# Two attention phases on one core: value products in groups of four tiles behind every second step, in place of two behind each

## The chip, the cores and the metric

One Trainium2 chip, one of its cores. The engines of the core run their own instruction lists and meet through semaphores: TensorE (PE in the profile, its weight loads apart as PEld), VectorE (DVE), ScalarE (ACT), GpSimd (POOL) and SyncE (SP), which issues the transfers. The metric is the time of one launch on the device in microseconds; lower is better.

## The reference, cut to what matters

Four layers run one after the other over x (16 batches of 256 tokens, width 128). Layers 0, 2 and 3 are attention layers with 16 heads of 8 channels; layer 1 is a mixture of three experts and is not touched here.

```python
# layers 0 and 3: self attention (256 keys), then cross attention (1601 keys) and an MLP
# layer 2: cross attention (1601 keys) with adaptive layer norms
attn_w = softmax(einsum('bhqd,bhkd->bhqk', q, k) * hd ** -0.5)
attn_out = einsum('bhqk,bhkd->bhqd', attn_w, v)
x = x + gate * (attn_out @ W_proj + b_proj)
```

All is computed in float32 and softmax runs over all keys.

## The kernel before, in words

`layers` calls five programs in a row: a small modulation stage, the attention phase `pa` (layer 0), the expert layer, and the attention phase `pb` (layers 2 and 3). This case is about `attention_phase`.

A phase carries two **streams**: "c", cross attention with 1601 keys (13 key tiles of 128, the last of 65), and "z", self attention with 256 keys (2 tiles). Each item of a stream is one batch of one layer. The phase is a list of **bodies**; each body does the scores and value products of one item of c and, where the streams overlap, one item of z, beside the preparation of later items and the finish of earlier ones. `pa` has 16 items each of c and z, z four bodies ahead: 12 bodies with both, 4 with c alone, 4 with z alone. `pb` has 32 items of c and 16 of z, z four bodies behind: 16 bodies with both, 16 with c alone.

The heads are taken in four **quads** of four. A quad is a row of **macro steps**: six of c with two key tiles each (tokens `("S", q, j, pp)`, two units per step), one of c for the last tile (`("T", q)`), and one of z (two tiles), eight steps in all or seven without z. The work around a step:

- *Scores* (S, T; L890, L898): four bf16 matmuls of 64 rows, two at a time on the two halves of the array, into one of two `aunit` buffers (`RING_A = 2`). ACT takes the exponential of the whole 128x1024 buffer into one of six `probs` buffers (L668) and so frees the `aunit`.
- *Value products* (V; L914): per key tile four products, one per head, each with 9 columns of weights (8 channels and a column of ones for the denominator) in its own strip of 32 columns of the array, against a 256 column float32 `probs`. Every product appears as two matmuls in the trace, so a tile is 8 of them. They add up in the bank `obank`, c in the left half and z in the right. The first tile of a quad waits until the quad before has been moved out: `wait(pe, o_ev, out_before[...])`, L905 of the kernel.
- *Moving out* (`oev`; L676): after the last tile of a quad ACT copies each stream's half of `obank` to `osb`.
- *Maxima* (M; L927 and L599): for the next item, PE computes the scores once more the other way round into one of three `dbank` buffers (`RING_D = 3`) and DVE reduces each to row maxima. 56 units of c and 8 of z per body, each of two buffers.
- *Helpers*: transposes of the context (`ctx`), key, query and value projections (`k`, `q`, `v`), output transposes (`o`), projections and the MLP, each once per item, in places given by hand.

The order is the same on every engine: `body_plan` gives each token a position between 0 and 1 in the body and sorts; `stage_list` repeats the plan for all bodies; every engine walks that list and does its share. In `body_plan` the list `main` holds score units (cost 1) and groups of values (cost: their number of tiles), spread evenly; the maxima units are spread evenly by their width on their own, and the helpers have fixed positions.

## Time and profile before

| | us |
|---|---|
| median of 3 runs | 5992.55 |
| lowest, highest | 5966.28, 6003.84 |
| the profiled execution | 5973.85 |
| its span | 5972.1 |

PE is busy 84% of the span, DVE 68%, ACT 62%. PE's busy time counts a matmul from its start to its end, while the next one is already streaming, so it is not a measure of how full the array is. In pb a body with both streams takes 99.3 us and one with c alone 88.6 us, from the first exponential of one to that of the next; the quads inside are unequal, since most helpers sit in the first two. In the rows below, windows show the busy time of each engine in a stretch, the timeline shows merged instructions in order of time with the idle time before them and what ended it, and the waits show who waited for whom.

### The profile page before, as it was taken

How to read it: one execution, taken by the hardware profiler on the slowest of the kernel's cores; microseconds unless marked ns; L12 is line 12 of the kernel's file. 1: busy time of each engine (PE TensorE's matmuls, PEld its weight loads, DVE VectorE, ACT ScalarE, POOL GpSimd, SP SyncE). 2: the span in 40 equal slices, each digit the busy share in tenths (PEclk: the TensorE clock that was granted, in tenths of full speed). 3: DMA queues.
4: the chain of work that ended last, by engine and by line, in shares of the span. 5: the costliest groups of instructions: out<-in, count | busy, mean ns of one | idle time of the engine just before them, and what ended most of it. 6: DMA issues, size and time to landing. Idle time of an engine off the chain costs nothing.

```text
span 5972.1 us, 124563 instructions
## 1 busy us (share of the span) xinstructions
PE 5013.7 (84%) x48593; PEld 2443.0 (41%) x48593; DVE 4034.0 (68%) x8799; ACT 3691.2 (62%) x5043; POOL 1624.9 (27%) x2594
## 2 busy tenths in 40 slices
PE   3688888888888688888598888888888898888887
PEld 1233333333433466666233333333334343333333
DVE  3487877777776233332588878787877777777774
ACT  1376767667767233332277777777777777777775
POOL 2434343343321000000423232323222322322321
PEclk8699999999999788888699999999999999999998
DMA  1221111211110100000211212121212111111110
GB/s 42 60 61 46 51 53 50 59 43 47 51 34 24 34 16 22 23 23 17 68 43 58 60 50 61 50 61 50 61 50 62 48 51 44 52 49 42 53 42 7
DMA packets 362968, 271.18 MB, mean 45 GB/s; under 512 B 47905, under 2 KB 324990, under 8 KB 362384
## 3 DMA queue, kind: packets, MB, share of 16 engines
q1 hardware_dynamic: 362384, 263.23, 15.5%
q8 instruction: 387, 6.34, 0.4%
q14 instruction: 197, 1.61, 0.1%
HBM read 86.96 MB, written 12.78 MB: 17 GB/s over the span
## 4 chain that ended last, share of the span: by engine, by line
PE 31%; DVE 8%; ACT 6%; POOL 4%; issue 4%; SPq 0%; DMA 0%; ACTq 0%; POOLq 0%
PE pb_obank L914 11%; PE pb_dbank L927 7%; DVE pb_c_maxs L599 6%; ACT pb_probs L668 4%; PE pb_aunit L890 4%; PE pb_aunit L961 2%; PE pb_aunit L968 2%; POOL pb_c_cin L789 1%; PE pb_aunit L1001 1%; PE pb_dbank L975 1%; DVE pb_z_maxs L599 1%; POOL pb_c_hg L852 1%; PE pb_aunit L995 1%; POOL pb_c_cs_y L785 0%; ACT pb_c_ksp L712 0%
## 5 line engine op out<-in xcount | busy, mean ns | idle before, releaser
L599 DVE TENSOR_REDUCE pb_c_maxs<-pb_dbank 128x1 f32<-128x512 f32 (+1 forms) x3584 | 2050.6, 627 | 633.3 <-PE pb_dbank L927 621.2
L668 ACT ACTIVATE pb_probs<-pb_aunit 128x1024 f32<-128x1024 f32 (+1 forms) x1792 | 1756.0, 1025 | 460.7 <-PE pb_aunit L890 364.6
L599 DVE TENSOR_REDUCE pa_c_maxs<-pa_dbank 128x1 f32<-128x512 f32 (+1 forms) x1792 | 1028.6, 627 | 395.6 <-PE pa_dbank L927 390.4
L668 ACT ACTIVATE pa_probs<-pa_aunit 128x1024 f32<-128x1024 f32 (+1 forms) x960 | 943.0, 1025 | 263.6 <-PE pa_aunit L890 190.8
L927 PE MATMUL pb_dbank<-pb_c_kst,pb_c_qst 62*128 62x512 bf16 (+1 forms) x4096 | 880.1, 343 | 141.5 <-DVE pb_c_maxs L599 77.0
L914 PE MATMUL pb_obank<-pb_probs,pb_c_vaug 128*9 128x256 f32 x13312 | 890.2, 382 | 6.6 <-ACT pb_probs L668 6.5
L890 PE MATMUL pb_aunit<-pb_c_qst,pb_c_kst 64*128 64x256 bf16 x6144 | 595.8, 273 | 53.3 <-ACT pb_probs L668 21.9
L927 PEld LDWEIGHTS pb_dbank<-pb_c_kst,pb_c_qst 62*128 62x128 bf16 x4096 | 248.6, 93 | 778.4 <-DVE pb_c_maxs L599 563.7
L927 PE MATMUL pa_dbank<-pa_c_kst,pa_c_qst 62*128 62x512 bf16 (+1 forms) x2048 | 449.0, 354 | 61.5 <-DVE pa_c_maxs L599 24.2
L914 PE MATMUL pa_obank<-pa_probs,pa_c_vaug 128*9 128x256 f32 x6656 | 461.2, 393 | 0.8 <-ACT pa_probs L668 0.7
L914 PEld LDWEIGHTS pb_obank<-pb_probs,pb_c_vaug 128*9 128x9 f32 x13312 | 276.1, 90 | 371.9 <-issue 177.3
L890 PEld LDWEIGHTS pb_aunit<-pb_c_qst,pb_c_kst 64*128 64x128 bf16 x6144 | 258.6, 95 | 242.0 <-ACT pb_probs L668 84.4
L890 PE MATMUL pa_aunit<-pa_c_qst,pa_c_kst 64*128 64x256 bf16 x3072 | 300.9, 278 | 25.7 <-ACT pa_probs L668 16.7
L927 PEld LDWEIGHTS pa_dbank<-pa_c_kst,pa_c_qst 62*128 62x128 bf16 x2048 | 123.3, 95 | 390.0 <-DVE pa_c_maxs L599 257.1
L599 DVE TENSOR_REDUCE pa_z_maxs<-pa_dbank 128x2 f32<-128x512 f32 x256 | 164.1, 686 | 115.3 <-PE pa_dbank L927 113.9
L1506 POOL TENSOR_TENSOR moe_xo<-moe_y,moe_xin 128x256 f32<-128x256 f32 x16 | 11.6, 723 | 844.2 <-DVE moe_y L1412 844.2
L914 PEld LDWEIGHTS pa_obank<-pa_probs,pa_c_vaug 128*9 128x9 f32 x6656 | 140.2, 91 | 195.7 <-issue 101.7
L803 POOL TENSOR_TENSOR pb_c_kf<-pb_c_kf,pb_c_ksp 128x1024 f32<-128x1024 f32 x64 | 114.3, 1787 | 311.1 <-ACT pb_c_ksp L712 311.1
L890 PEld LDWEIGHTS pa_aunit<-pa_c_qst,pa_c_kst 64*128 64x128 bf16 x3072 | 129.1, 96 | 117.3 <-ACT pa_probs L668 44.2
L599 DVE TENSOR_REDUCE pb_z_maxs<-pb_dbank 128x2 f32<-128x512 f32 x256 | 164.6, 685 | 10.5 <-PE pb_dbank L927 8.7
L1564 PE MATMUL moe_bank_f<-moe_diag,moe_pr 128*128 128x128 f32 (+1 forms) x832 | 136.9, 320 | 35.5 <-DVE moe_pt L1255 28.5
L1456 ACT ACTIVATE moe_pr<-moe_bank_s,moe_nm 128x400 f32<-128x400 f32 (+1 forms) x128 | 74.3, 594 | 132.5 <-DVE moe_nm L1337 132.5
(460 smaller groups left out, 6864.7 us busy)
## 6 DMA issues: line engine op xcount, KB each, us to landing
pb_c_kst<-pb_c_ksp SPq DMA_DIRECT2D x384, 200.1 KB
pa_c_kst<-pa_c_ksp SPq DMA_DIRECT2D x192, 200.1 KB
pb_c_cin<-in_ctx SPq DMA_DIRECT2D x32, 768.0 KB
pa_c_cin<-in_ctx SPq DMA_DIRECT2D x16, 768.0 KB
moe_cin<-in_ctx SPq DMA_DIRECT2D x16, 768.0 KB
pb_c_qst<-pb_c_qsp SPq DMA_DIRECT2D x384, 32.0 KB
pa_z_qst<-pa_z_qsp SPq DMA_DIRECT2D x192, 32.0 KB
pa_z_kst<-pa_z_ksp SPq DMA_DIRECT2D x192, 32.0 KB
```

The source lines that it names most:

```text
L599: dve.tensor_reduce(dst, dbank[N % RING_D][:, 0:cnt * width].rearrange("p (s c) -> p s c", s=cnt), AX.X, ALU.max).then_inc(d_free, 1)
L668: act.activation(probs[u % RING_P][0:rows].rearrange("p a i q -> p (a i q)"), src[0:rows, :], ACT.Exp, scale=HD ** -0.5).then_inc(a_free, 1)
L789: pool.tensor_scalar(s.cin[0:rows, t, :], s.cin[0:rows, t, :], s.cs_m[0:rows, t:t + 1], s.cs_y[0:rows, t:t + 1], ALU.add, ALU.mult).then_i ...
L803: pool.tensor_tensor(s.kf[:, part], s.kf[:, part], s.ksp[:, 0, part], ALU.subtract).then_inc(s.k_r, 1)
L852: pool.tensor_tensor(s.hg[:], s.hg[:], s.z[:], ALU.mult).then_inc(s.g_p, 1)
L890: ins = pe.matmul(dst[:, par * 512 + h * NQ:par * 512 + (h + 1) * NQ], s.kst[b2][lo:lo + ROWS, pair, t * P:(t + 1) * P], s.qst[b2][lo:lo + ...
L914: ins = pe.matmul(obank[32 * h4:32 * h4 + HD + 1, half * NQ:(half + 1) * NQ], s.vaug[i % 2][:, t, 4 * q + h4, :], src, start=(t == 0), sto ...
L927: ins = pe.matmul(dbank[nd[tok, s.key, i, par] % RING_D][:, col:col + width], s.qst[b2][lo:lo + MAX_ROW, p, qt * P:(qt + 1) * P], s.kst[b2 ...
L961: ins = pe.matmul(dst[:, at - t0 * P:at - t0 * P + width], w.wkp[:], src[:, at:at + width], start=True, stop=True)
L968: ins = pe.matmul(dst[0:rows, (t - t0) * P:(t - t0 + 1) * P], (s.srct if s.has_ctx else s.xmt)[:, t * P:t * P + rows], w.wv[:], start=True ...
L1456: act.activation(pr[qt][:, at:at + width], sbank[c][:, 0:width], ACT.Exp, bias=nm[:, qt:qt + 1], scale=D ** -0.5, accum_out=sums[:, qt, c: ...
L1564: ins = pe.matmul(dst[0:rows, (t - t0) * P:(t - t0 + 1) * P], pr[qt][:, t * P:t * P + rows], diag[qt][:], start=True, stop=True)
```

## The change

The group of values that stood behind the scores of each macro step (those of the step before) now stands behind the scores of every second step only and holds the values of the two steps before it. At even steps there is none. With eight steps a quad, the four groups of a quad hold: the two z tiles of the quad before and c's tiles 0 and 1; tiles 2 to 5; tiles 6 to 9; tiles 10 to 12. The tokens that move `obank` out (`oev`) stay right behind the last values of their quad, and so come to stand between the z tiles and tile 0 of the next quad. Nothing else is edited; the number of instructions is the same (17525 rows on PE in both).

```diff
--- before.py
+++ after.py
@@ -235,13 +235,16 @@
     for m, (s, units, _, _) in enumerate(macros):
         main += [[(s, 0, t)] for t in units]
         costs += [1.0] * len(units)
-        prev, _, vals, ends = macros[m - 1]
-        off = 0 if m else -1
-        group = [(prev, off, t) for t in vals]
-        if ends is not None:
-            group += [(o, off, ("oev", ends)) for o in streams]
-        main.append(group)
-        costs.append(len(vals))
+        group = []
+        for back in ((2, 1) if m % 2 else ()):
+            prev, _, vals, ends = macros[m - back]
+            off = 0 if m >= back else -1
+            group += [(prev, off, t) for t in vals]
+            if ends is not None:
+                group += [(o, off, ("oev", ends)) for o in streams]
+        if group:
+            main.append(group)
+            costs.append(sum(1 for g in group if g[2][0] == "V"))
     for pos, group in spread(main, 0.0, 1.0, costs):
         marks += [(pos, item) for item in group]
 
```

Place 1, PE, at the border of two quads in a body of pb with both streams. `pb_obank` is the bank of the values, `pb_aunit` takes scores, `pb_dbank` maxima. Before:

```order
L914 MATMUL pb_obank<-pb_probs2,pb_z_vaug1 9x256 x2
L914 MATMUL pb_obank<-pb_probs3,pb_z_vaug1 9x256 x2
L914 MATMUL pb_obank<-pb_probs2,pb_z_vaug1 9x256 x2
L914 MATMUL pb_obank<-pb_probs3,pb_z_vaug1 9x256 x2
L927 MATMUL pb_dbank0<-pb_c_kst0,pb_c_qst0 128x512
L927 MATMUL pb_dbank1<-pb_c_kst0,pb_c_qst0 128x512
L890 MATMUL pb_aunit1<-pb_c_qst0,pb_c_kst0 128x256 x4
L890 MATMUL pb_aunit0<-pb_c_qst0,pb_c_kst0 128x256 x4
L975 MATMUL pb_dbank2<-pb_ident,pb_c_osb 128x128 x4
L927 MATMUL pb_dbank0<-pb_c_kst0,pb_c_qst0 128x512
L927 MATMUL pb_dbank1<-pb_c_kst0,pb_c_qst0 128x512
L914 MATMUL pb_obank<-pb_probs4,pb_c_vaug0 9x256 x2
```

Now (the lines of the kernel have moved down by three, so L914 is L917 and so on):

```order
L893 MATMUL pb_aunit1<-pb_c_qst0,pb_c_kst0 128x256 x4
L893 MATMUL pb_aunit0<-pb_c_qst0,pb_c_kst0 128x256 x4
L930 MATMUL pb_dbank0<-pb_c_kst0,pb_c_qst0 128x512
L930 MATMUL pb_dbank1<-pb_c_kst0,pb_c_qst0 128x512
L917 MATMUL pb_obank<-pb_probs2,pb_z_vaug1 9x256 x2
L917 MATMUL pb_obank<-pb_probs3,pb_z_vaug1 9x256 x2
L917 MATMUL pb_obank<-pb_probs2,pb_z_vaug1 9x256 x2
L917 MATMUL pb_obank<-pb_probs3,pb_z_vaug1 9x256 x2
L917 MATMUL pb_obank<-pb_probs4,pb_c_vaug0 9x256 x2
L917 MATMUL pb_obank<-pb_probs5,pb_c_vaug0 9x256 x2
L917 MATMUL pb_obank<-pb_probs4,pb_c_vaug0 9x256 x2
L917 MATMUL pb_obank<-pb_probs5,pb_c_vaug0 9x256 x2
```

The z tiles and the next quad's tiles 0 and 1, which had two maxima units and two score units between them, are now neighbours, and the score units have gone ahead of both.

Place 2, ACT, at the same border; `osb` is what `obank` is moved to. Before:

```order
L668 ACTIVATE pb_probs4<-pb_aunit1 128x1024
L668 ACTIVATE pb_probs5<-pb_aunit0 128x1024
L676 ACTIVATE pb_c_osb<-pb_obank 128x256
L676 ACTIVATE pb_z_osb<-pb_obank 128x256
L668 ACTIVATE pb_probs0<-pb_aunit1 128x1024
L668 ACTIVATE pb_probs1<-pb_aunit0 128x1024
```

Now:

```order
L671 ACTIVATE pb_probs4<-pb_aunit1 128x1024
L671 ACTIVATE pb_probs5<-pb_aunit0 128x1024
L671 ACTIVATE pb_probs0<-pb_aunit1 128x1024
L671 ACTIVATE pb_probs1<-pb_aunit0 128x1024
L679 ACTIVATE pb_c_osb<-pb_obank 128x256
L679 ACTIVATE pb_z_osb<-pb_obank 128x256
L671 ACTIVATE pb_probs2<-pb_aunit1 128x1024
```

The two moves out stood behind the two exponentials of the quad's first step; they now stand behind all four of its first two steps.

Place 3, PE, in the middle of a quad of the same phase. Before:

```order
L890 MATMUL pb_aunit1<-pb_c_qst0,pb_c_kst0 128x256 x4
L914 MATMUL pb_obank<-pb_probs3,pb_c_vaug0 9x256 x2
L914 MATMUL pb_obank<-pb_probs4,pb_c_vaug0 9x256 x2
L914 MATMUL pb_obank<-pb_probs3,pb_c_vaug0 9x256 x2
L914 MATMUL pb_obank<-pb_probs4,pb_c_vaug0 9x256 x2
L927 MATMUL pb_dbank0<-pb_c_kst1,pb_c_qst1 128x512
L927 MATMUL pb_dbank1<-pb_c_kst1,pb_c_qst1 128x512
L890 MATMUL pb_aunit0<-pb_c_qst0,pb_c_kst0 128x256 x4
L890 MATMUL pb_aunit1<-pb_c_qst0,pb_c_kst0 128x256 x4
L927 MATMUL pb_dbank2<-pb_c_kst1,pb_c_qst1 128x512
L927 MATMUL pb_dbank0<-pb_c_kst1,pb_c_qst1 128x512
L914 MATMUL pb_obank<-pb_probs5,pb_c_vaug0 9x256 x2
```

Now:

```order
L893 MATMUL pb_aunit1<-pb_c_qst0,pb_c_kst0 128x256 x4
L930 MATMUL pb_dbank2<-pb_c_kst1,pb_c_qst1 128x512
L930 MATMUL pb_dbank0<-pb_c_kst1,pb_c_qst1 128x512
L917 MATMUL pb_obank<-pb_probs3,pb_c_vaug0 9x256 x2
L917 MATMUL pb_obank<-pb_probs4,pb_c_vaug0 9x256 x2
L917 MATMUL pb_obank<-pb_probs3,pb_c_vaug0 9x256 x2
L917 MATMUL pb_obank<-pb_probs4,pb_c_vaug0 9x256 x2
L917 MATMUL pb_obank<-pb_probs5,pb_c_vaug0 9x256 x2
L917 MATMUL pb_obank<-pb_probs0,pb_c_vaug0 9x256 x2
L917 MATMUL pb_obank<-pb_probs5,pb_c_vaug0 9x256 x2
L917 MATMUL pb_obank<-pb_probs0,pb_c_vaug0 9x256 x2
L930 MATMUL pb_dbank1<-pb_c_kst1,pb_c_qst1 128x65
```

Two groups of four rows with scores and maxima between them have become one of eight; the maxima that stood between now stand all on the other side.

## Rows read from the trace of the kernel before

**Rows 1.** windows, four quads of one body with both streams; columns in the first line.

```profile
core 0: us, PE busy (x) PEld busy (x) DVE busy (x) ACT busy (x) POOL busy (x), PEclk, DMA share, GB/s
3999.80:4029.90 30.10, 26.82 (x285) 13.61 (x281) 24.14 (x63) 20.13 (x29) 7.37 (x15) 1.00 0.37 111
4029.90:4057.90 28.00, 23.11 (x249) 9.76 (x244) 19.60 (x48) 21.37 (x29) 17.34 (x33) 1.00 0.05 15
4057.90:4079.10 21.20, 19.34 (x228) 7.61 (x228) 18.14 (x33) 16.51 (x21) 6.16 (x5) 1.00 0.28 75
4079.10:4099.10 20.00, 18.23 (x228) 7.16 (x224) 18.68 (x36) 15.78 (x19) 1.14 (x6) 1.00 0.04 9
```

**Rows 2.** windows, four quads of one body with the long stream alone.

```profile
5248.20:5272.50 24.30, 22.05 (x237) 10.91 (x232) 18.00 (x41) 16.33 (x22) 6.67 (x14) 1.00 0.36 114
5272.50:5298.80 26.30, 21.51 (x222) 9.40 (x217) 17.49 (x32) 19.69 (x25) 8.25 (x9) 1.00 0.00 1
5298.80:5319.50 20.70, 18.44 (x212) 8.33 (x208) 16.00 (x30) 14.67 (x18) 9.10 (x9) 1.00 0.24 64
5319.50:5336.80 17.30, 15.90 (x193) 5.93 (x190) 16.03 (x31) 13.11 (x16) 0.57 (x3) 1.00 0.04 9
```

**Rows 3.** timeline, last quad of rows 1; columns: start, length, engine, work, idle before.

```profile
4079.10 1.94 ACT L668 ACTIVATE pb_probs<-pb_aunit 128x1024 f32<-128x1024 f32 x2 [0.27 <-PE pb_aunit L890]
...
4079.73 0.55 PEld L914 LDWEIGHTS pb_obank<-pb_probs,pb_z_vaug 128*9 128x9 f32 x16 [0.23 <-issue]
...
4080.71 0.10 PEld L927 LDWEIGHTS pb_dbank<-pb_c_kst,pb_c_qst 62*128 62x128 bf16 x2 [0.43 <-DVE pb_c_maxs L599]
...
4080.92 0.39 ACT L676 ACTIVATE pb_c_osb<-pb_obank 128x256 f32<-128x256 f32 x1
...
4081.14 2.48 DVE L599 TENSOR_REDUCE pb_c_maxs<-pb_dbank 128x1 f32<-128x512 f32 x4 [0.22 <-PE pb_dbank L927]
4081.18 0.41 ACT L676 ACTIVATE pb_z_osb<-pb_obank 128x256 f32<-128x256 f32 x1
...
4081.88 0.09 PEld L927 LDWEIGHTS pb_dbank<-pb_c_kst,pb_c_qst 62*128 62x128 bf16 x1 [0.52 <-DVE pb_c_maxs L599]
...
4082.20 1.05 PE L914 MATMUL pb_obank<-pb_probs,pb_c_vaug 128*9 128x256 f32 x16
4083.18 0.12 PEld L927 LDWEIGHTS pb_dbank<-pb_z_kst,pb_z_qst 62*128 62x128 bf16 x4 [0.43 <-DVE pb_c_maxs L599]
...
4083.61 1.29 DVE L599 TENSOR_REDUCE pb_z_maxs<-pb_dbank 128x2 f32<-128x512 f32 x2
```

**Rows 4.** waits, the last two quads of rows 1: waiter, awaited, us, times, longest.

```profile
PEld pb_dbank L927 <- DVE pb_c_maxs L599: 12.3, 29, 1.0
...
DVE pb_c_maxs L599 <- PE pb_dbank L927: 4.1, 9, 1.6
```

**Rows 5.** waits, the first two quads of rows 1.

```profile
DVE pb_c_maxs L599 <- PE pb_dbank L927: 13.3, 12, 2.1
```

**Rows 6.** timeline of weight loads, a visit of one tile and the load after it.

```profile
4097.71 0.12 PEld L914 LDWEIGHTS pb_obank<-pb_probs,pb_c_vaug 128*9 128x9 f32 x8 [0.23 <-issue]
4098.26 0.09 PEld L927 LDWEIGHTS pb_dbank<-pb_c_kst,pb_c_qst 62*128 62x128 bf16 x1 [0.43 <-DVE pb_c_maxs L599]
```

**Rows 7.** instructions of tile pb_obank: count, ns min/median/max, first and last start.

```profile
L914 PE MATMUL pb_obank<-pb_probs,pb_z_vaug x1024: 379/379/385, 3332.7 to 4887.3; 128*9 128x256 f32 x171
```

**Rows 8.** the page, part 5: the exponentials of pb.

```profile
L668 ACT ACTIVATE pb_probs<-pb_aunit 128x1024 f32<-128x1024 f32 (+1 forms) x1792 | 1756.0, 1025 | 460.7 <-PE pb_aunit L890 364.6
```

**Rows 9.** waits, the last two quads of rows 2.

```profile
DVE pb_c_maxs L599 <- PE pb_dbank L927: 5.6, 10, 2.5
```

**Rows 10.** windows, nine bodies of pa with both streams.

```profile
306.00:1301.00 995.00, 865.18 (x9187) 385.41 (x9183) 757.60 (x1646) 700.88 (x920) 370.69 (x620) 0.96 0.19 53
```

**Rows 11.** timeline of the second quad of rows 1, around the key projection.

```profile
4051.45 1.98 PE L961 MATMUL pb_aunit<-pb_c_srct,pb_l_cross_wkp 128*128 128x512 f32 x4
...
4053.78 1.29 DVE L599 TENSOR_REDUCE pb_c_maxs<-pb_dbank 128x1 f32<-128x512 f32 x2 [2.15 <-PE pb_dbank L927]
```

## The prediction

> **What bounds the kernel now.** First the windows, quad by quad. In the last quad of a body with both streams DVE is busy 18.68 of 20.00 us, 93%, while PE shows 91% and ACT 79% [rows 1]; with c alone it is DVE 16.03 of 17.30 us, again 93% [rows 2]. In the third quads DVE has 86% and 77%, in the first 80% and 74%, in the second 70% and 66% [rows 1, 2]. So the late quads are bound by the maxima on DVE, and the early ones partly by PE, which does the helpers there. Next the timeline, for how tight the ring of three maxima buffers is [rows 3]. PE loads the last maxima before a visit to the values at 4081.88, after waiting 0.52 us for DVE; the visit starts at 4082.20, the next maxima load follows at 4083.18, and DVE starts on that buffer at 4083.61. Its earlier run of four, begun at 4081.14 and 2.48 long, ended at 4083.62. The slack is zero: three buffers carry DVE over a visit of two tiles and no further. Last the waits: in these two quads PE's loads wait 12.3 us for DVE (29 times) and DVE only 4.1 us for PE [rows 4]; in the first two quads DVE waits 13.3 us, 12 times [rows 5].
>
> **What a visit costs.** A visit of two tiles takes 4080.71 - 4079.73 = 0.98 us from its first load to the next load of other work [rows 3], one of one tile 4098.26 - 4097.71 = 0.55 [rows 6]. So a tile is 0.43 us and leaving costs 0.12. Before a visit the weight loads idle 0.23 us without a cause [rows 3, 6], part of it under the maxima still streaming. The fixed price of a visit lies between 0.12 and 0.35; I take 0.2, the middle.
> The Trainium skill, "TensorEngine Tiling (Array Packing)", Key Properties, says that changing the tiling mode drains the engine; scores, maxima and values use different tilings here, and these idle times agree with it. By that rule alone the change is a gain, and it is the first rival below.
>
> **What goes.** A body with both streams has 32 visits and will have 16; with c alone 28 and 16. The z values of pb run from 3332.6 to 4887.1 [rows 7], 16 bodies; with pa's 12 that is 28 bodies with both streams and 4 + 16 = 20 with c alone. Removed: 28 x 16 + 20 x 12 = 688 visits, 138 us at 0.2 (83 to 241). This is a gain only where PE is the limit. The matmuls, exponentials and reductions stay as many. Where PE waits for DVE anyway, a shorter PE time is worth nothing.
>
> **What comes, in the middle of a quad.** The visit of four tiles takes 0.12 + 4 x 0.43 = 1.84 us, 0.86 more than now. The maxima between two visits are twice as many, but only three buffers can be ahead, so DVE stands idle 0.86 us behind each visit of four (two a quad) and 0.43 behind the one of three, wherever it is the limit. The scores that now go ahead do not help: they need the `aunit` buffers, not DVE. The exponentials stay off the path: two pairs of them need some 4 x 0.92 us and the wait through the visit, about 5.1 us for two steps, against 8 x 0.62 + 0.86 = 5.8 on DVE.
>
> **What comes, at the border of two quads.** Tile 0 of the next quad now stands directly behind the z tiles, and between them lie only the moves out of `obank` on ACT, for which PE must wait. Now that wait is hidden by maxima and scores. In the trace the move of c starts 4080.92 - 4079.73 = 1.19 us after the z visit began, that of z at 4081.18 and ends 0.41 later, 1.86 us after the visit began [rows 3]. Then tiles 0 and 1 take their 0.98, so the next maxima come 2.84 us after the visit's start in place of 0.98: DVE idles 1.86 us more, and PE itself 1.86 - 0.86 = 1.0. ACT does not make it shorter, because the moves now stand behind four exponentials, whose starts are 0.92 apart (two take 1.94 [rows 3], one 1.02 [rows 8]); the last pair is released only as PE reaches the z visit. With c alone there are no z tiles: the move of c comes 3 x 0.92 = 2.76 us after the start of the first step's last exponential and takes 0.39; PE arrives at about 2.1 (that exponential 1.02 [rows 8], scores 0.2, two maxima buffers at DVE's pace). The wait is about 1.0 us.
>
> **The sum per body.** Both streams, late quads: 1.86 + 2 x 0.86 + 0.43 = 4.0 each, 8.0 for two; of the 4.1 us that DVE waits there now [rows 4] half goes with the visits removed: +6.0. Early quads, where PE is half the limit: -8 x 0.2 = -1.6 for the visits, +2.0 for the two waits at the borders, and half of the starvation, (4 x 0.86 + 2 x 0.43) / 2 = 2.15: +2.6. Together +8.6 us. With c alone, late: 2 x (1.0 + 1.72 + 0.43) = 6.3, less 2.1 of the 5.6 that DVE waits now [rows 9]: +4.2. Early, DVE busy 70% only: -6 x 0.2 + 2.0 + a third of 4.3: +2.2. Together +6.4. For pa I take the prices of pb, since DVE is busy 757.60 of 995 us there, 76% [rows 10], against 81% over the four quads of rows 1.
> Total: 28 x 8.6 + 20 x 6.4 = 241 + 128 = 369 us. The profiled execution took 5973.85 us and has its span of 5972.1 and 1.75 around it; with 369 that is 6343. The median of the runs stands 19 us above that execution, 0.3%, less than any bound here. **Forecast: 6345 us, 6% slower.**
> Bounds of this case: all idle in the late quads goes with the visits, none is added in the early ones, and a visit's fixed part is 0.35: 8.0 - 4.1 + 2.0 - 2.8 = 3.1 and 6.3 - 5.6 + 2.0 - 2.1 = 0.6 a body, 99 us, 6075. None of the idle goes, the early quads pay in full and the fixed part is 0.12: 13.3 and 11.9 a body, 610 us, 6585.
>
> **Rivals.**
> *PE is the limit and the visits were the cost (ends faster).* The place is every border between values and other work. If DVE's waits for PE are what sets the time and the borders of quads are covered, 688 visits at 0.2 come off: 5974 - 138 = 5836. For it: PE shows the highest share everywhere, and DVE waits for PE 13.3 us in the early quads. Against it: PE's loads wait for DVE 12.3 us in the late quads, and the wait for the moves out follows from the order alone. It decides once a body gains more on PE than 6 us. Chance 0.08.
> *Helpers and values come apart (no change).* Some of DVE's longest waits come where a visit stands beside a helper: the key projection, 1.98 us on PE, lies directly behind a visit, and DVE waits 2.15 us there [rows 11]. In the new order maxima stand between them. If six of the 12 waits of the early quads [rows 5] lose a visit's 0.98, 5.9 us a body go: 2.7 and 0.5 are left, 86 us; with the fixed part at 0.35 another 103 us go: 5974 + 86 - 103 = 5957. Against it: a visit of four is itself as long as a helper. Chance 0.10.
> *The forecast's case*, 0.82: DVE starved behind the long visits, PE waiting at the borders.
>
> **How the numbers follow.** A measurement of this kernel tells 1%, 60 us, from no change. Slower by more takes the whole of the forecast's case, 0.82; within 1% the second rival, 0.10; faster 0.08. The range reaches down to 6000, into the no-change case and below the lower bound, since how much idle is absorbed is the least sure term, and up to 6500, because all the terms at their worst at once is unlikely. Left out are the faster case and about a tenth at the ends.
>
> **What would show it.** Visits of 16, 24 and 32 matmuls to `obank`, 16 a body, the long ones 1.84 us from first load to next load. At every border a wait of PE for the `osb` moves of 1 us or so (now nearly none), 192 of them in all. DVE's waits for PE in the late quads up from 4.1 to about 10 us, and its share there down from 93% to about 80%, the busy time the same. The quads of rows 1 longer by some 3 us in the late half and 1 in the early. Wrong would be: late quads no longer (DVE did not starve, slack was larger than it looks), early quads shorter by more than 1 us each (the second rival, or the first), or no wait for the moves out.

## The result: 14.3% slower, 857 us where 369 were forecast

| | before | after |
|---|---|---|
| median, us | 5998.19 (4 runs) | 6855.9 (4 runs) |
| lowest, highest | 5966.28, 6018.63 | 6849.05, 6859.31 |
| profiled execution's span | 5972.1 | 6857.5 |
| from first to last exponential of pa | 1842 | 2089 |
| between the phases | 1016 | 1035.5 |
| from first to last exponential of pb | 2977 | 3596 |
| PE's granted clock at half, added up | 765 | 1197 |

The ratio is 1.143, with a 95% interval of 1.140 to 1.146. The direction was forecast, the size was not: 6856 lies far above the range's end of 6500. Both phases pay; the expert layer between them does not. The work is the same: both profiles count 48593 matmuls on PE. The kernel before was run again beside every group of experiments, with medians of 5981 to 6000 us, so differences under some 20 us are not read below. A time "a body" is a mean over ten bodies of pb with both streams, or nine with c alone, unless a place is named.

The page of the changed kernel, part 5 (columns: work and count, busy us, mean ns, idle us before it and what ended most of it):

```profile
L602 DVE TENSOR_REDUCE pb_c_maxs<-pb_dbank 128x1 f32<-128x512 f32 (+1 forms) x3584 | 2055.2, 626 | 1114.3 <-PE pb_dbank L930 1103.4
L671 ACT ACTIVATE pb_probs<-pb_aunit 128x1024 f32<-128x1024 f32 (+1 forms) x1792 | 1734.1, 1026 | 1038.8 <-PE pb_aunit L893 789.8
...
L917 PE MATMUL pb_obank<-pb_probs,pb_c_vaug 128*9 128x256 f32 x13312 | 891.5, 407 | 126.4 <-ACT pb_c_osb L679 75.7
```

The exponentials take as long as before, and the idle time ahead of them has gone from 460.7 us [rows 8] to 1038.8. The forecast had an entry for DVE's idle time and none for this one.

The windows over the four quads of the body that answers to rows 1 (columns as there):

```profile
4484.70:4517.00 32.30, 27.73 (x284) 13.80 (x281) 23.85 (x62) 20.36 (x28) 7.37 (x15) 1.00 0.36 107
4517.00:4551.30 34.30, 25.94 (x256) 11.02 (x251) 19.74 (x48) 21.50 (x28) 18.44 (x34) 0.95 0.03 8
4551.30:4576.80 25.50, 19.68 (x228) 7.83 (x224) 18.13 (x33) 16.18 (x19) 5.14 (x4) 1.00 0.24 62
4576.80:4604.10 27.30, 20.80 (x228) 7.57 (x225) 18.68 (x35) 15.40 (x19) 1.14 (x6) 0.94 0.03 8
```

DVE and ACT do what they did [rows 1], the quads are 2.2, 6.3, 4.3 and 7.3 us longer, and the granted clock, 1.00 in all four before, is 0.95 and 0.94 in two. DVE's share of the last quad is 68%.

The border of two quads, timeline of the same body (start, length, engine, work, idle before):

```profile
4576.93 3.77 ACT L671 ACTIVATE pb_probs<-pb_aunit 128x1024 f32<-128x1024 f32 x4 [1.64 <-PE pb_aunit L893]
...
4578.00 0.11 PEld L893 LDWEIGHTS pb_aunit<-pb_c_qst,pb_c_kst 64*128 64x128 bf16 x4 [0.68 <-ACT pb_probs L671]
...
4578.92 0.12 PEld L893 LDWEIGHTS pb_aunit<-pb_c_qst,pb_c_kst 64*128 64x128 bf16 x4 [0.80 <-ACT pb_probs L671]
...
4579.04 0.10 PEld L930 LDWEIGHTS pb_dbank<-pb_c_kst,pb_c_qst 62*128 62x128 bf16 x2
...
4579.46 0.55 PEld L917 LDWEIGHTS pb_obank<-pb_probs,pb_z_vaug 128*9 128x9 f32 x16 [0.32 <-issue]
...
4579.57 1.29 DVE L602 TENSOR_REDUCE pb_c_maxs<-pb_dbank 128x1 f32<-128x512 f32 x2 [0.82 <-PE pb_dbank L930]
4580.58 0.39 ACT L679 ACTIVATE pb_c_osb<-pb_obank 128x256 f32<-128x256 f32 x1
4580.86 0.39 ACT L679 ACTIVATE pb_z_osb<-pb_obank 128x256 f32<-128x256 f32 x1
4581.30 0.55 PEld L917 LDWEIGHTS pb_obank<-pb_probs,pb_c_vaug 128*9 128x9 f32 x16 [1.29 <-ACT pb_z_osb L679]
...
4582.71 1.29 DVE L602 TENSOR_REDUCE pb_c_maxs<-pb_dbank 128x1 f32<-128x512 f32 x2 [1.86 <-PE pb_dbank L930]
```

Two things stand here. The second: tile 0 starts 4581.30 - 4579.46 = 1.84 us after the z visit, and DVE stands idle 1.86 us; that is the forecast's chain (1.86 us) within 0.02 us. The first was not forecast: four score units in a row need `aunit` buffers of which there are two. The loads of the third and the fourth wait 0.68 and 0.80 us for ACT (the matmuls themselves 0.38 and 0.52), and the maxima at 4579.04, which have a free buffer, stand behind them in PE's own list. DVE is idle 0.82 us before the visit has begun.

The middle of the quad before, timeline, at full clock:

```profile
4563.65 1.41 PEld L917 LDWEIGHTS pb_obank<-pb_probs,pb_c_vaug 128*9 128x9 f32 x32 [0.23 <-ACT pb_probs L671]
...
4565.49 0.11 PEld L930 LDWEIGHTS pb_dbank<-pb_c_kst,pb_c_qst 62*128 62x128 bf16 x4 [0.43 <-DVE pb_c_maxs L602]
...
4565.77 1.73 DVE L602 TENSOR_REDUCE pb_c_maxs<-pb_dbank 128x2 f32<-128x130 f32 x4 [0.70 <-PE pb_dbank L930]
...
4566.00 3.77 ACT L671 ACTIVATE pb_probs<-pb_aunit 128x1024 f32<-128x1024 f32 x4 [1.55 <-PE pb_aunit L893]
```

The visit of four tiles is 4565.49 - 4563.65 = 1.84 us long, as forecast, and DVE idles 0.70 for it (0.86). ACT idles 1.55. The same place in the next quad:

```profile
4587.58 3.54 PE L917 MATMUL pb_obank<-pb_probs,pb_c_vaug 128*9 128x256 f32 x32
...
4591.04 0.11 PEld L930 LDWEIGHTS pb_dbank<-pb_c_kst,pb_c_qst 62*128 62x128 bf16 x4 [0.78 <-issue]
...
4591.31 0.49 DVE L602 TENSOR_REDUCE pb_c_maxs<-pb_dbank 128x2 f32<-128x130 f32 x2 [2.33 <-PE pb_dbank L930]
...
4591.54 3.77 ACT L671 ACTIVATE pb_probs<-pb_aunit 128x1024 f32<-128x1024 f32 x4 [3.38 <-PE pb_aunit L893]
```

The same 32 matmuls take 3.46 us to the next load. The windows before, over and behind them:

```profile
4576.80:4587.50 10.70, 7.64 (x78) 2.55 (x73) 7.90 (x16) 7.55 (x10) 0.57 (x3) 1.00 0.01 2
4587.58:4591.03 3.45, 3.45 (x33) 1.06 (x32) 1.41 (x3) 0.58 (x1) 0.00 (x0) 0.52 0.00 0
4591.10:4604.10 13.00, 9.55 (x122) 3.90 (x120) 9.29 (x17) 7.20 (x9) 0.57 (x3) 1.00 0.06 16
```

The granted clock falls to half, 1.2 of 2.4 GHz, over the whole visit, after 10.7 us in which PE was busy 71%; before the change it was busy 91% over this quad [rows 1] and the clock stayed up. The Trainium skill, "TensorE: Matmul & The Clock Gate", A second HAM failure mode, says that small idle gaps between groups of matmuls can make the clock swing between its two levels. The rows agree: the longest idle time between matmuls in this quad is 0.79 us.

With c alone, border of two quads:

```profile
6082.11 0.12 PEld L893 LDWEIGHTS pb_aunit<-pb_c_qst,pb_c_kst 64*128 64x128 bf16 x4 [0.80 <-ACT pb_probs L671]
...
6082.81 1.29 DVE L602 TENSOR_REDUCE pb_c_maxs<-pb_dbank 128x1 f32<-128x512 f32 x2 [0.87 <-PE pb_dbank L930]
6083.75 0.42 ACT L679 ACTIVATE pb_c_osb<-pb_obank 128x256 f32<-128x256 f32 x1
6084.22 0.13 PEld L917 LDWEIGHTS pb_obank<-pb_probs,pb_c_vaug 128*9 128x9 f32 x8 [1.89 <-ACT pb_c_osb L679]
6084.22 1.90 PE L917 MATMUL pb_obank<-pb_probs,pb_c_vaug 128*9 128x256 f32 x16 [1.44 <-ACT pb_c_osb L679]
...
6086.69 2.48 DVE L602 TENSOR_REDUCE pb_c_maxs<-pb_dbank 128x1 f32<-128x512 f32 x4 [2.59 <-PE pb_dbank L930]
```

```profile
6084.22:6086.12 1.90, 1.90 (x18) 0.52 (x20) 0.00 (x0) 0.00 (x0) 0.00 (x0) 0.50 0.00 0
```

The loads wait 1.89 us where 1.0 was forecast, the visit of two tiles behind the wait takes 1.90 us for 1.05 [rows 3], since the granted clock is 0.50 over it (the window), and DVE loses 0.87 + 2.59 us. Last the waits over the whole span, loads of `obank` for a move out (us, times, longest):

```profile
PEld pb_obank L917 <- ACT pb_c_osb L679: 100.9, 63, 2.0
PEld pb_obank L917 <- ACT pb_z_osb L679: 86.5, 64, 1.7
...
PEld pa_obank L917 <- ACT pa_z_osb L679: 64.5, 49, 1.7
...
PEld pa_obank L917 <- ACT pa_c_osb L679: 22.7, 15, 2.0
```

They are 191 waits, where the forecast had 192. In the kernel before there are 6 such waits, 1.7 us in all.

### The profile page after: what moved, and what is told of

Its sections match the earlier page's. It is cut to its first block, busy times and chain, and to the rows that moved or that the text cites. A ratio compares the mean times of both kernels' runs of the same rounds, so it can differ in the third digit from the quotient of the medians.

```text
span 6857.5 us, 124563 instructions
## 1 busy us (share of the span) xinstructions
PE 5295.1 (77%) x48593; PEld 2555.4 (37%) x48593; DVE 4029.9 (59%) x8799; ACT 3669.8 (54%) x5043; POOL 1627.7 (24%) x2594
## 4 chain that ended last, share of the span: by engine, by line
PE 28%; ACT 11%; DVE 8%; issue 7%; POOL 0%; SPq 0%; DMA 0%; ACTq 0%; POOLq 0%; DVEq 0%
PE pb_obank L917 12%; ACT pb_probs L671 9%; DVE pb_c_maxs L602 6%; PE pb_dbank L930 6%; PE pb_aunit L893 2%; PE pb_aunit L971 2%; PE pb_aunit L964 2%; DVE pb_z_maxs L602 1%; PE pb_aunit L956 1%; ACT pb_c_ksp L715 1%; PE pb_dbank L978 1%; PE pb_aunit L998 1%; PE pb_aunit L1004 1%; ACT pb_z_osb L679 0%; PE pb_aunit L988 0%
## 5 line engine op out<-in xcount | busy, mean ns | idle before, releaser
L671 ACT ACTIVATE pb_probs<-pb_aunit 128x1024 f32<-128x1024 f32 (+1 forms) x1792 | 1734.1, 1026 | 1038.8 <-PE pb_aunit L893 789.8
L930 PE MATMUL pb_dbank<-pb_c_kst,pb_c_qst 62*128 62x512 bf16 (+1 forms) x4096 | 949.7, 354 | 202.6 <-DVE pb_c_maxs L602 151.8
L917 PE MATMUL pb_obank<-pb_probs,pb_c_vaug 128*9 128x256 f32 x13312 | 891.5, 407 | 126.4 <-ACT pb_c_osb L679 75.7
L893 PE MATMUL pb_aunit<-pb_c_qst,pb_c_kst 64*128 64x256 bf16 x6144 | 651.9, 283 | 228.3 <-ACT pb_probs L671 169.1
L930 PE MATMUL pa_dbank<-pa_c_kst,pa_c_qst 62*128 62x512 bf16 (+1 forms) x2048 | 476.3, 354 | 103.5 <-DVE pa_c_maxs L602 68.6
L917 PEld LDWEIGHTS pb_obank<-pb_probs,pb_c_vaug 128*9 128x9 f32 x13312 | 327.1, 94 | 563.2 <-issue 139.5
L917 PE MATMUL pa_obank<-pa_probs,pa_c_vaug 128*9 128x256 f32 x6656 | 439.0, 402 | 56.1 <-ACT pa_z_osb L679 38.2
L893 PEld LDWEIGHTS pb_aunit<-pb_c_qst,pb_c_kst 64*128 64x128 bf16 x6144 | 244.6, 97 | 495.1 <-ACT pb_probs L671 356.0
L893 PE MATMUL pa_aunit<-pa_c_qst,pa_c_kst 64*128 64x256 bf16 x3072 | 323.0, 281 | 124.7 <-ACT pa_probs L671 87.9
L917 PEld LDWEIGHTS pa_obank<-pa_probs,pa_c_vaug 128*9 128x9 f32 x6656 | 162.2, 93 | 275.7 <-issue 67.0
```

The lines of the kernel that those rows point to most:

```text
L671: act.activation(probs[u % RING_P][0:rows].rearrange("p a i q -> p (a i q)"), src[0:rows, :], ACT.Exp, scale=HD ** -0.5).then_inc(a_free, 1)
L893: ins = pe.matmul(dst[:, par * 512 + h * NQ:par * 512 + (h + 1) * NQ], s.kst[b2][lo:lo + ROWS, pair, t * P:(t + 1) * P], s.qst[b2][lo:lo + ...
L917: ins = pe.matmul(obank[32 * h4:32 * h4 + HD + 1, half * NQ:(half + 1) * NQ], s.vaug[i % 2][:, t, 4 * q + h4, :], src, start=(t == 0), sto ...
L930: ins = pe.matmul(dbank[nd[tok, s.key, i, par] % RING_D][:, col:col + width], s.qst[b2][lo:lo + MAX_ROW, p, qt * P:(qt + 1) * P], s.kst[b2 ...
```

## The experiments

Four theories. **A**, the border: z values, the moves out, tile 0 in a chain. **B**, the long visit: three `dbank` buffers do not carry DVE over 1.84 us. **C**, the row of scores: four score units in a row on two `aunit` buffers make PE wait for ACT, with the maxima held behind them. **D**, the clock that falls behind such waits. "Border" below is everything in steps 0 and 1 of a quad, "middle" the rest.

### 1 and 2: middle and border apart

`e1_border_back`: middle changed, border as before.

```diff
-        for back in ((2, 1) if m % 2 else ()):
+        for back in {0: (1,), 1: (1,), 3: (2, 1), 5: (2, 1), 7: (2, 1)}.get(m % 8, ()):
```

> The changed kernel, but at the border of two quads the values stand as they did before the change (z tiles and moves out behind the first step, c's tiles 0 and 1 behind the second); tiles 2 to 5, 6 to 9 and 10 to 12 stay in groups. Theory A (the border costs most, by the chain z values, moves out, tile 0, and by the four score units ahead of it): the steps 0 and 1 of a quad lost 11 us a body with both streams and 5 to 8 with c alone, together some 450 us, and they come back: about 6410 us. Theory B (long visits starve the maxima wherever they are): only a quarter of the long visits goes, so about a quarter of the 857 us: about 6640 us.

6351.69 against 5981.27 us, 1.061 (1.058 to 1.064): +370.

`e2_border_only`: border changed, middle as before.

```diff
-        for back in ((2, 1) if m % 2 else ()):
+        for back in {0: (), 1: (2, 1)}.get(m % 8, (1,)):
```

> The kernel before, with the change made at the borders alone: z tiles, moves out and c's tiles 0 and 1 in one group behind the second step's scores, all other values behind each step as before. Theory A: about 5998 + 450 = 6450 us. Theory B: about 6200 us. If the two halves (this and the run with the border as before) add up to the whole change, their losses sum to 857 us; if they sum to clearly less, there is a loss that only both together bring, such as a lower clock.

6472.35 us, 1.081 (1.078 to 1.084): +491. The parts add up over the run, 370 + 491 = 861 of 857, though less well by kind of body in pb: 7.9 + 10.0 of 20.5 us with both streams, 8.2 + 15.6 of 16.6 with c alone. Which part is paid where shifts from kernel to kernel; the split below holds for the run as a whole, and only as far as parts can be added up. Theory A had 6410 us on record for e1 and 6450 for e2, B 6640 and 6200: both runs lie by A's, e1 58 us under it. The forecast had about 240 for the border (28 x 5.72 + 20 x 4.0) and 129 for the rest: twice and three times too little.

### 3 and 13: order of the scores, and length of the visit

`e3_split_visits`: the change's order of scores, but the values of the two steps are two groups, which `spread` sets apart.

```diff
-        group = []
         for back in ((2, 1) if m % 2 else ()):
...
-            group += [(prev, off, t) for t in vals]
+            group = [(prev, off, t) for t in vals]
...
-        if group:
             main.append(group)
-            costs.append(sum(1 for g in group if g[2][0] == "V"))
+            costs.append(len(vals))
```

> The changed kernel's order of scores (four score units, then four tiles), but each group of four tiles is split into two visits of two tiles with one maxima unit between them, the moves out in front of that unit at the border. Theory B (the length of a visit starves DVE: 1.84 us against a ring that lasts 0.98): visits have the old length, DVE is fed between them, and most of the loss inside the quads goes, 5 to 9 us a body: 6450 to 6600 us. Theory C (the four score units in a row wait for the two score buffers, and the maxima behind them come late): the order of scores is unchanged, the extra visits cost 0.2 us each where PE is the limit: 6750 us or more.

6468.62 against 5981.27 us, 1.081 (1.078 to 1.083): +487, 387 less than the change.

`e13_row_of_scores_only`: e3 with the border as before.

```diff
-        for back in ((2, 1) if m % 2 else ()):
+        for back in ({0: (1,), 1: (1,)}.get(m % 8, (2, 1) if m % 2 else ())):
```

> Inside the quads the scores of two steps stand in a row as in the change, but their four tiles go in two visits of two with one maxima unit between; the borders are as before the change. Against the variant with the same borders and visits of four (6352 us, 370 over the kernel before). Theory C (four score units in a row are the loss, two score buffers): most of the 370 us stays, 6250 to 6350 us. Theory B (the length of the visit is the loss): 60 to 150 us over the kernel before, 6050 to 6150 us.

6183.82 against 5991.14 us, 1.032 (1.029 to 1.036): +193. So the middle's 370 are 193 for the four score units in a row, with visits of two tiles as before, and 177 for the double length. At the border it is 487 - 193 = 294 and 491 - 294 = 197. More than half of the loss, 487 us, comes almost without long visits: e3 has 1456 visits, ten of them of four tiles, the kernel before 1466.

The 294 us are not the row of scores alone. In e3 the moves out still stand behind four exponentials, and tile 0 still waits for them (loads, whole span):

```profile
PEld pb_obank L915 <- ACT pb_c_osb L677: 37.6, 48, 2.0
PEld pb_obank L915 <- ACT pb_z_osb L677: 36.4, 48, 0.8
```

With pa's it is 145 waits and 113 us, against 191 and 275 in the change. How the 294 fall to A and C no run shows. Nor did either theory have these times on record: C had 6750 us or more for e3 and B 6450 to 6600; for e13 C had 6250 to 6350 and B 6050 to 6150, and 6184 lies between. Both are at work in the middle, in nearly equal parts. Where the maxima stand differs too between visits that are split and visits that are not.

### 4: the moves out earlier

`e4_early_move_out`: c's move stands behind its own last tile, one for z behind z's.

```diff
+            if vals[0][2] == prev.kt - 1:
+                group.append((prev, off, ("oev", vals[0][1])))
             if ends is not None:
-                group += [(o, off, ("oev", ends)) for o in streams]
+                group.append((prev, off, ("oev", ends)))
```

> The changed kernel, with c's half of the value bank moved out right behind c's last tile instead of behind the z tiles of the next quad; z's move stays. In bodies with c alone no wait for a move is left at the border; with both streams the chain is one move (0.28 us) shorter. Theory A: c alone gains 1 to 1.5 us at each of 80 borders, both streams 0.3 at each of 112: 110 to 150 us, about 6725 us. Theory C (scores in a row are what delays the border): the wait only changes its name, less than 40 us: above 6815 us.

6655.01 against 5981.27 us, 1.112 (1.109 to 1.114): 201 less than the change. With c alone the border has no chain left:

```profile
5858.87 0.39 PE L895 MATMUL pb_aunit<-pb_c_qst,pb_c_kst 64*128 64x256 bf16 x4 [0.52 <-ACT pb_probs L673]
5858.99 0.10 PEld L932 LDWEIGHTS pb_dbank<-pb_c_kst,pb_c_qst 62*128 62x128 bf16 x2
...
5859.41 0.55 PEld L919 LDWEIGHTS pb_obank<-pb_probs,pb_c_vaug 128*9 128x9 f32 x16 [0.32 <-issue]
...
5859.52 1.29 DVE L604 TENSOR_REDUCE pb_c_maxs<-pb_dbank 128x1 f32<-128x512 f32 x2 [0.87 <-PE pb_dbank L932]
```

The wait of 1.89 us is gone and the four borders of a pb body with c alone are 0.0, 0.91, -0.37 and -0.04 us longer than before, where the change has 3.06, 1.88, 0.81 and 2.09. With both streams nothing moved (+20.0 us a body against +20.5), since z's own move stays in the chain. Theory A is shown for c alone: 9.4 us a body are left of 16.6. A part of the gain is the clock's, since the time at half speed falls from 1197 to 935 us. DVE's 0.87 ahead of the visit stays: that part is C's.

### 5 and 6: DVE relieved

`e5_before_half_reduce` is the kernel before, `e6_change_half_reduce` the change, both with this:

```diff
-dbank[N % RING_D][:, 0:cnt * width]
+dbank[N % RING_D][:, 0:cnt * width // (2 if cnt == 1 else 1)]
```

> The kernel before, with each reduction of a 512 column maxima buffer reading only its first 256 columns (part of the maxima is left out); its time is to be compared with the next run, not with the kernel before. DVE loses about 0.27 us on each of some 5376 reductions. Where DVE set the late quads they now go at the pace of exponentials and PE: about 8 us a body less, near 5600 us.

> The changed kernel with the same half reductions. Theory B (DVE starved behind the long visits is the loss inside the quads): DVE now has room to catch up, so that part, some 370 us, nearly goes, and only the loss at the borders stays: 400 to 500 us over the run before it. Theory C (the chain of scores, two score buffers and exponentials sets the pace in both): DVE's work does not matter and the whole 14% stays, 750 us or more over the run before it.

5726.44 against 5988.15 us, 0.956 (0.953 to 0.959), and 6575.55, 1.098 (1.094 to 1.101). The first 256 of the 512 columns are read, and the rest of the maxima is left out. With the reductions at 399 ns in place of 627 the change still costs 849 us. So B alone is refuted: with 36% less time in each reduction DVE had room to catch up, and 8 of 857 us came back. The page has, for e5:

```profile
L668 ACT ACTIVATE pb_probs<-pb_aunit 128x1024 f32<-128x1024 f32 (+1 forms) x1792 | 1750.5, 1025 | 345.2 <-PE pb_aunit L890 266.2
```

and for e6:

```profile
L671 ACT ACTIVATE pb_probs<-pb_aunit 128x1024 f32<-128x1024 f32 (+1 forms) x1792 | 1730.9, 1026 | 908.3 <-PE pb_aunit L893 655.6
```

ACT's idle time grows by 563 us in pb, as between the two whole kernels (578). So there is a second limit beside DVE, at nearly its pace: e5 itself is only 262 us faster than the kernel before. The wait for the moves out is untouched by this edit (275 us of loads in e6 as in the change), so these two runs do not tell C from A.

### 9, 10 and 11: both rings relieved

Beside the reduction, each exponential from the seventh on is cut to half its columns, so that the other half of `probs` keeps old values.

```diff
+                    n_e = 1024 if u < RING_P else 512
...
-"p a i q -> p (a i q)"), src[0:rows, :], ACT.Exp,
+"p a i q -> p (a i q)")[:, 0:n_e], src[0:rows, 0:n_e], ACT.Exp,
```

> The kernel before with half reductions (first 256 of 512 columns) and half exponentials (first 512 of the 1024 columns of a score buffer, after the first six): DVE and ACT are both relieved, PE has all its work. It is the base for the next two runs. PE alone should set it: its columns streamed and switches come to some 80 us a body, so about 5300 to 5500 us.

> The changed kernel with both halved. Theory B or C or both (inside the quads DVE and the exponentials take turns as the limit, each idle behind a long visit): with both relieved that part goes and only the borders' wait for the moves out stays: 250 to 450 us over the run before. Rival (PE itself lost time, by its clock or by something in the long visits): 700 us or more over the run before it.

> The variant with the border as before and groups of four only inside the quads, both halved. With full work it was 370 us slower than the kernel before. If the switches between values and other work are a real price (0.2 us each, 12 visits a body fewer, 48 bodies) and PE is now the limit, this is faster than the first run of this call by up to 110 us. If PE's price of a visit is nothing: equal. If the loss inside the quads is PE's own: still 300 us slower.

Against 5999.72 us: e9 5558.57, 0.926 (0.923 to 0.929); e10, the change, 5943.87, 0.990 (0.987 to 0.993); e11, e1's middle, 5705.11, 0.950 (0.947 to 0.954). The change costs 385 us over e9 where it cost 857, its middle 147 where it cost 370, and the border 385 - 147 = 238 where it cost 491. So more than half of the loss, 472 us, goes once the exponentials are short as well as the reductions. That both rings have to be tight for it is not shown, since short exponentials with full reductions were not run. They also bring the moves out forward, so part of the 472 is A's.

What is left is a wait of PE itself, and not of the clock: PE's idle time is 1094 us in e10 and 750 in e9 (span less busy time), 344 of the 385, and the time at half speed is shorter, 552 us against 659. Of the 344, 149 are matmuls that wait for a move out, 191 times; in e9 no matmul does. No gain of the merged visits shows here either: e11 has 570 fewer than e9 and is 147 us slower.

### 7 and 12: maxima between the scores

With a room of 0.1 for every group of values the score units spread evenly, and maxima come between them. `e7_maxima_between` is the change with it:

```diff
-            costs.append(sum(1 for g in group if g[2][0] == "V"))
+            costs.append(0.1)
...
-            at(0.050, -1, "o", 0)
+            at(0.070, -1, "o", 0)
```

> The changed kernel, with a group of values taking almost no room in the spread (cost 0.1 in place of its tiles), so that the maxima units lie between the score units instead of around the visits; one output transpose moves from 0.050 to 0.070 to stay behind the move out. Theory C (maxima held up behind four score units): DVE gets a buffer between any two score units, gain of 2 to 4 us a body, 6650 to 6760 us. Theory B (only the length of the visit counts): the visits are as long, and a score unit stands between the last maxima and the visit, so nothing is gained: 6850 us or up to 100 us more.

`e12_before_maxima_between` is the kernel before with the same two values.

```diff
-        costs.append(len(vals))
+        costs.append(0.1)
```

> The kernel before with a group of values taking almost no room in the spread (cost 0.1), so that maxima units lie between the score units as in the seventh run, which gained 230 us on the changed kernel. If that gain came from feeding DVE while the scores wait for the exponentials, the kernel before, where visits of two already fit the ring, gains little or nothing: 5950 to 6030 us. If maxima between scores are better whatever the visits: 5800 to 5900 us.

e7: 6626.22 against 5988.15 us, 1.106 (1.103 to 1.109), 230 less than the change. e12: 6075.55 against 5999.72, 1.011 (1.009 to 1.014), 76 more than before. The same edit gains where scores are bunched and loses where they are not, as C has it; the loss was not expected (5950 to 6030 us on record). It mends a quarter of the change's loss only.

### 8: twice the maxima matmuls

`e8_maxima_twice`: the change, PE computes each block of maxima twice, so it has more to do and idles less.

```diff
+                            for _ in range(2):
-                            ins = pe.matmul(dbank[...
+                                ins = pe.matmul(dbank[...
```

> The changed kernel with every maxima matmul issued twice, the second over the first, 0.1 to 0.2 us of PE work a buffer that changes no value. Theory D (PE's clock drops in the new idle time and costs 150 to 200 us): PE is less idle, the granted clock rises from 0.913 to 0.93 or more, and the place that ran at half speed in every body (a visit of four tiles of 3.46 us) takes 1.84; where DVE is starved the extra work costs 0.2 us a buffer, so the total stays within 100 us of 6856. Rival: the clock is no cause but a companion, it stays as it is and the time rises by the extra work, 200 to 500 us.

7046.11 against 5988.15 us, 1.176 (1.172 to 1.180). The time at half the clock fell from 1197 to 704 us, below the 765 of before, and still the kernel is 190 us slower than the change, where at most 100 were expected. The last two quads of the body:

```profile
4664.24:4691.63 27.39, 23.02 (x268) 9.88 (x264) 18.27 (x33) 16.36 (x19) 4.84 (x4) 1.00 0.22 58
4691.63:4718.98 27.35, 22.63 (x268) 9.22 (x264) 18.73 (x35) 15.60 (x20) 1.14 (x6) 1.00 0.03 9
```

The last quad has 40 matmuls more and takes the same 27.3 us, at clock 1.00: its steps 2 and 3, where the slow visit stood, are 0.85 us longer than before in place of 2.26. But the edit changed the work as well.

The trace of the change itself holds the cleaner comparison, the last quads of two bodies with the same instructions:

```profile
4815.85:4843.19 27.34, 20.83 (x228) 7.61 (x224) 18.71 (x36) 15.41 (x20) 1.14 (x6) 0.94 0.03 8
4938.25:4964.31 26.06, 19.19 (x228) 7.31 (x224) 18.71 (x36) 15.40 (x20) 1.14 (x6) 1.00 0.03 8
```

In the second the clock did not fall, and the visit of 32 matmuls took 1.91 us in place of 3.54. The quad is 1.28 us shorter, for 3.4 us less at half speed: 38%. What D costs in all stays an estimate: 1197 - 765 = 432 us more at half speed, at 38% for the quad or 47% for a visit alone (3.46 us for 1.84), would be some 160 to 200 us. It is contained in the parts above. No run held the clock up over the whole kernel and left all else alone.

Where it falls can be read from the traces. The time at half speed is 735 us in e13 and 791 in e1, which change the middle, but 1030 in e2, which changes the border, and 886 in e3. So nearly all of D belongs to the border: by the same shares 100 to 125 us of e2's 491, and 10 to 12 of e1's 370. In pb a body with c alone spends 18.5 us at half speed, with 3.7 before (mean of 15 bodies).

### 14 and 18: what a visit costs

Both are e9 with a room of 2 per tile. `e18_pairs_same_spread` keeps the groups of two:

```diff
-        costs.append(len(vals))
+        costs.append(2.0 * len(vals))
...
-            at(0.050, -1, "o", 0)
+            at(0.070, -1, "o", 0)
```

`e14_single_tile_visits` makes every tile a group:

```diff
-        group = [(prev, off, t) for t in vals]
+        parts = [[(prev, off, t)] for t in vals]
         if ends is not None:
-            group += [(o, off, ("oev", ends)) for o in streams]
-        main.append(group)
-        costs.append(len(vals))
+            parts[-1] += [(o, off, ("oev", ends)) for o in streams]
+        main += parts
+        costs += [2.0] * len(vals)
```

> The kernel before with both halved (5559 us), and with each tile of the values as a group of its own, so that where a maxima unit falls between the two tiles of a pair, one visit becomes two; the trace says how many. About 15 more visits a body, 700 in all. If a visit's fixed price is 0.2 us on PE's path, the time rises by about 140 us; if it is near 0.12, the part that the trace showed on leaving, by 85; if PE's waits cover it, by less than 40. By the forecast's reading the saving of the change was worth 138 us to PE, so this run tells whether that term was real.

> The kernel before with both halved, pairs kept, and each group with the room of the single-tile run (2 per tile, the output transpose at 0.070). Against the single-tile run (5519 us) only the split of visits differs, 768 of them. If a visit's fixed part of 0.12 to 0.35 us is on the path, this run is 90 to 270 us faster than that one: 5250 to 5430 us. If shorter visits let PE feed the other engines sooner and that outweighs it: 5519 us or more.

e14: 5518.77 against 5991.14 us, 0.922 (0.917 to 0.926). e18: 5619.92 against 5999.53, 0.937 (0.934 to 0.940). The trace of e14 has 2234 visits to `obank`, that of e9 1466: 768 more visits are 101 us faster at the same room, and 40 faster than e9. At the forecast's 0.2 us they would have cost 154. The tiles also stand at other places among the maxima, so this bounds the price of a visit and does not measure it. The page of e14:

```profile
L915 PE MATMUL pb_obank<-pb_probs,pb_c_vaug 128*9 128x256 f32 x13312 | 968.3, 382 | 3.7
L915 PEld LDWEIGHTS pb_obank<-pb_probs,pb_c_vaug 128*9 128x9 f32 x13312 | 232.8, 89 | 384.2 <-issue 213.3
```

and of e18:

```profile
L915 PE MATMUL pb_obank<-pb_probs,pb_c_vaug 128*9 128x256 f32 x13312 | 889.6, 382 | 3.6
L915 PEld LDWEIGHTS pb_obank<-pb_probs,pb_c_vaug 128*9 128x9 f32 x13312 | 276.1, 90 | 370.3 <-issue 142.2
```

With half as many visits again the loads' idle time without a cause grows by 71 us (213.3 for 142.2) in a kernel that is 101 us shorter: idle time shown on the loads is not time lost. Why single tiles gain is not shown. The room matters too: e18 is 61 us slower than e9, with the same groups (and the output transpose at 0.070).

### 15: long visits only beside helpers

`e15_grouped_beside_helpers`: the kernel before, in phase pa alone, with three pairs of groups joined where a helper stands.

```diff
+        joined = (5, 7, 13) if streams[-1].lead > 0 else ()
+        group = []
+        for back in (() if m + 1 in joined else (2, 1) if m in joined else (1,)):
```

> The kernel before with groups only in phase pa and only at three places a body, where the quads with groups got shorter although the visits are long: tiles 6 to 9 and 10 to 12 of the first quad, tiles 6 to 9 of the second. In the run with the borders as before these places changed by -0.87, -0.23 and -2.26 us a body. Twelve bodies: 40 us less than the kernel before, 0.7%, if places add up. If a place only pushes its wait into the next one (the next place there was 1.84 slower), no difference within 15 us.

5979.83 against 5991.14 us, 0.998 (0.996 to 1.000): no difference that can be told, where 40 us were expected if the places add up. It tests the second rival's mechanism in pa only, at 48 places.

### 16 and 17: the other direction

The kernel before, all work whole, with e14's single tiles and its output transpose at 0.070: `e16_single_tiles_wide` at a room of 2.0 a tile, `e17_single_tiles_narrow` at 1.0.

```diff
+        main += parts
+        costs += [2.0] * len(vals)
```

> The kernel before with full work, each tile of values a group of its own with room 2 in the spread, so that most pairs are split by a maxima unit. Theory C and B turned round (short visits keep DVE and the exponentials fed): DVE waited 22 us a body for PE; up to 2 us of it goes, 5850 to 5950 us. If the visits' fixed price is on the path where PE is the limit: up to 150 us slower, 6000 to 6140 us.

> As the run before it, with room 1 a tile, which leaves the maxima units where they are in the kernel before but for those that now fall between two tiles; fewer pairs are split. Same sign as the wide one and about half its size: 5920 to 5980 us by theories B and C, up to 6070 us by the fixed price.

e16: 5914.12 against 5999.53 us, 0.986 (0.984 to 0.989), 85 us faster than before and 942 than the change. e17: 5953.92, 0.993 (0.990 to 0.995). The narrow room was expected to split fewer pairs; the trace has 2541 visits, against 2234 in e16 and 1466 before. So 1075 more visits at the room of before are 46 us faster, where 0.2 us each would have cost 215. The third and fourth quads of e16's body with both streams:

```profile
4010.82:4032.07 21.25, 19.64 (x224) 7.28 (x224) 18.21 (x33) 16.29 (x21) 6.16 (x5) 1.00 0.28 75
4032.07:4052.10 20.03, 18.70 (x224) 7.21 (x224) 18.29 (x35) 15.67 (x20) 1.14 (x6) 1.00 0.04 9
```

They are as long as before [rows 1]; DVE was tight there already. The gain lies in pb's bodies with c alone (2.2 us each) and in pa (5.3 each for three with c alone, 1.6 with both).

## Why the prediction was wrong, step by step

- **What bounds the kernel now.** "The late quads are bound by the maxima on DVE" was half of it. DVE had the highest share, but halving its work left 849 of 857 us of loss (e5, e6). The other half is PE's own order: it waits for ACT's ring of two buffers and for the moves out, and what stands behind waits with it. With both engines relieved 385 us stay.
- **"The exponentials stay off the path: ... about 5.1 us for two steps".** This step failed most. It compared totals of two engines over two steps and not the order in which PE serves them. Four score units on two buffers wait 0.68 and 0.80 us, and the maxima behind them wait too, though their buffer is free: DVE idles 0.82 us ahead of the border. The order of scores alone is 193 us in the middle (e13); at the border it is a part of the 294 (e3 less e13), which hold the moves out behind four exponentials as well. The forecast had nothing for it.
- **The long visit.** Right as a length (1.84 us) and nearly as idle time of DVE (0.70 for 0.86). By differences of runs the length is worth 177 + 197 us over the kernel, clock included.
- **The border with both streams.** The chain of 1.86 us was right (1.84 us). That the early quads pay 1.0 was wrong: they were taken as half bound by PE, but steps 0 and 1 are 2.65, 3.25, 2.51 and 2.57 us longer in the four quads. 11.0 us a body stand against 5.7.
- **The border with c alone.** Forecast 1.0, measured 1.89 for the loads, with 0.87 + 2.59 us of DVE behind it; 7.8 us a body against 4.0. It starts from four exponentials in a row and ends in a visit of almost twice its length, at a granted clock of 0.50. That the move out is the awaited link is shown by e4.
- **What goes with the visits.** Counted right (688 forecast, 683 in the trace, 1466 to 783), priced wrong. The 0.2 us do not show as time (e14, e18, e17). The drain rule that the prediction took from the Trainium skill, "TensorEngine Tiling (Array Packing)", Key Properties, may hold, but no rival can be built on it here.
- **"Of the 4.1 us that DVE waits there now half goes".** DVE's waits in the late quads went to 14.0 us, 10 times, where about 10 were forecast; which of the old 4.1 are among them the trace does not tell.
- **Omitted: the clock.** Rows 1 and 2 have it at 1.00, and the text took it to stay. 432 us more at half the clock are worth some 160 to 200 by the estimate at e8. It amplifies what the order begins, at the border above all.
- **The body as a sum.** Both streams in pb +20.5 us (border 11.0, middle 9.5) against 8.6, c alone +16.6 (7.8, 8.7) against 6.4; in pa +15.5 (nine bodies) and +12.4 (three). The second quad alone is 6.3 us longer, where 1 was forecast.
- **The rivals.** Both on the other side fell with the result itself. Fewer visits gain nothing (e11, e14, e17, e18), and joining them at helpers gained nothing in pa (e15).
- **The range.** Its upper bound, 6585, took each term at its worst, but only the terms of the list; a ring left out and a clock held fixed lie outside any such bound. The direction came out as forecast, but only in part by the forecast's mechanism: 193 us of the loss (e13) come from the row of scores alone, which it had set aside.

Not settled: how the border's 294 us are shared between the row of scores and the wait for the moves out, whether short exponentials alone would have taken back what both did, and why single tiles gain.

## What to carry to other kernels

Where one in-order engine feeds two consumers through two small rings, lay out its list and walk both rings through it: bunching the work for one ring blocks the other, and neither share of busy time shows it. Before merging short pieces into long ones, ask whether the switch between them is on the path; here the opposite, finer pieces spread wider, was the faster kernel. And when an edit makes TensorE wait often, price its work at half the clock as the upper bound.

## What the runs showed of the hardware

- TensorE's clock went to half without any long pause. In a quad whose gaps between matmuls were at most 0.79 us, after 10.7 us in which PE was busy 71%, 32 matmuls took 3.54 us for 1.92, at a granted clock of 0.52; in the same place of another body it stayed up and they took 1.91 us. Over the run the time at half rose from 765 to 1197 us, and doing useless matmuls in the gaps brought it to 704 (e8).
- Leaving and entering a group of matmuls of another tiling shows 0.12 and 0.23 us in the trace [rows 6], by the prediction's reading, and a kernel with 768 more such changes was 101 us faster (e18 to e14), one with 1075 more 46 us (before to e17): idle time shown on the loads need not be time.
- Halving the columns of a reduction took it from 627 to 399 ns, of an exponential from 1025 to 597.
